# Experts' stage of a perceiver kernel: the routing weight multiplied into the result, and the routing placed between the first units

## The reference

```python
scores = einsum('btd,de->bte', x, router_w)
probs = softmax(scores)
routing_weights, routing_idx = top_k(probs, 2)
routing_weights = routing_weights / sum(routing_weights)
expert_w = einsum('btke,btk->bte', one_hot, routing_weights)
gate = einsum('bted,edf->btef', dispatched, gate_proj)
up = einsum('bted,edf->btef', dispatched, up_proj)
acts = silu(gate) * up
expert_out = einsum('btef,efd->bted', acts, down_proj)
return einsum('bted,bte->btd', expert_out, expert_w)
```

## Time and profile before

| | us |
|---|---|
| median of 3 runs | 3089.42 |
| lowest and highest | 3085.68, 3090.41 |
| the profiled execution, its own time | 3081.74 |
| its span, first to last instruction | 3080.0 |
| busy in the span: PE, DVE, ACT, POOL | 2488.2, 2267.4, 1868.9, 902.2 |
| mean granted TensorE clock | 0.882 of 2.4 GHz |

### The profile page before, as it was taken

The page is one execution under the profiler, slowest core; times in us unless marked ns, Lnnn a source line. Parts: engine busy times, 40 slices in busy tenths (PEclk is TensorE's granted clock), DMA queues, the critical chain, the costliest instruction groups (busy, mean ns, idle before and its releaser), DMA issues. The chain is left out here.

```text
span 3080.0 us, 35217 instructions
## 1 busy us (share of the span) xinstructions
PE 2488.2 (81%) x11867; PEld 1402.0 (46%) x11875; DVE 2267.4 (74%) x3046; ACT 1868.9 (61%) x2572; POOL 902.2 (29%) x498
## 2 busy tenths in 40 slices
PE   6699999998899999999999999954366641435998
PEld 3366666663344444444444444322355521423665
DVE  4487777754999999999999999855899921534443
ACT  4365555545888888888888889842455520013443
POOL 1021111111444444444444444300200031102665
PEclk9899999999999999999999999975667775557999
DMA  1000000001000000000000000000011013010000
GB/s 53 11 25 15 18 18 14 14 8 69 1 0 35 1 35 0 34 0 35 0 34 0 35 0 0 0 11 16 10 35 34 21 36 49 5 29 33 16 16 14
DMA packets 17732, 60.16 MB, mean 20 GB/s; under 512 B 1520, under 2 KB 10032, under 8 KB 15664
## 3 DMA queue, kind: packets, MB, share of 16 engines
q1 hardware_dynamic: 17584, 58.29, 6.2%
HBM read 53.04 MB, written 5.24 MB: 19 GB/s over the span
## 5 line engine op out<-in xcount | busy, mean ns | idle before, releaser
L251 PE MATMUL a_ps<-a_x,a_w 128*128 128x512 f32 x1536 | 695.6, 598 | 24.7 <-DVE a_kf L599 12.4
L251 PEld LDWEIGHTS a_ps<-a_x,a_w 128*128 128x128 f32 x1536 | 291.5, 191 | 404.3 <-issue 367.8
L774 POOL TENSOR_TENSOR a_den<-a_qf,a_ksum 128x1024 f32<-128x1024 f32 x128 | 271.2, 2119 | 510.2 <-DVE a_qf L592 473.5
L777 POOL TENSOR_TENSOR a_num<-a_qf,a_kvsum 128x1024 f32<-128x1024 f32 x128 | 295.0, 2304 | 186.1 <-DVE a_kvsum L617 186.0
L2137 DVE TENSOR_REDUCE x_rn<-x_sqk 128x8 f32<-128x512 f32 x256 | 174.3, 681 | 104.8 <-ACT x_sqk L2061 100.6
L2061 ACT ACTIVATE x_sqk<-x_b_k 128x512 f32<-128x512 f32 x256 | 153.1, 598 | 155.8 <-PE x_b_k L1973 149.3
L262 PE MATMUL a_ps<-a_att,a_w 128*128 128x512 f32 x480 | 215.8, 592 | 0.0
L592 DVE SCALAR_TENSOR_TENSOR a_qf<-a_eq,a_qf 128x1024 f32<-128x1024 f32 x128 | 195.4, 1526 | 1.7
L1954 POOL TENSOR_TENSOR x_kn<-x_craw,x_w 128x256 f32<-128x256 f32 x64 | 47.1, 736 | 509.7 <-DVE x_craw L2126 488.1
L445 ACT ACTIVATE a_den<-a_den,consts 128x1024 f32<-128x1024 f32 x128 | 147.0, 1149 | 57.3 <-POOL a_den L774 57.3
L599 DVE SCALAR_TENSOR_TENSOR a_kf<-a_ek,a_ps 128x1024 f32<-128x1024 f32 x128 | 155.5, 1215 | 27.8 <-ACT a_ps L441 23.1
(11 more groups left out here) (417 smaller groups left out, 5480.3 us busy)
## 6 DMA issues: line engine op xcount, KB each, us to landing
a_w<-layers SPq DMA_DIRECT2D x8, 2577.0 KB, 9.2
x_craw<-ctx SPq DMA_DIRECT2D x32, 256.0 KB, 2.6
y_cx<-ctx_t SPq DMA_DIRECT2D x16, 512.0 KB, 3.2
m_w<-experts SPq DMA_DIRECT2D x8, 608.0 KB, 3.8
x_w<-xattn_w SPq DMA_DIRECT2D x1, 2048.0 KB, 7.3
x_all<-x_t SPq DMA_DIRECT2D x1, 1024.0 KB, 4.9
t_scratch<-t_tmp SPq DMA_DIRECT2D x1, 1024.0 KB, 3.9
t_q<-t_scratch SPq DMA_DIRECT2D x4, 256.0 KB
```

The lines of the kernel that those rows point to most:

```text
L251: last = nc.tensor.matmul(bank(tile, j), col(par, part * HK + u * P, P), x[:, t0:t0 + BANK], start=True, stop=True)
L774: nc.gpsimd.tensor_tensor(by_batch(den[:, b, :]), by_batch(qf[:, b, :]), bcast(ksum[:, b, :], S), ALU.mult).then_inc(d_ready, 1)
L777: nc.gpsimd.tensor_tensor(by_batch(num[:, b, :]), by_batch(qf[:, b, :]), bcast(kvsum[:, b, :], S), ALU.mult).then_inc(n_ready, 1)
```

## The change

Seven things are done, all in `l1_moe` and its packing of weights.

1. The weight is multiplied into the result. `output(k)` on VectorE is now two instructions: `m_share` = `tile_o` x `m_wb` (L1284), then `x_all` += `m_share` (L1286), with a wait between. `spread`, `weigh`, `m_xw` and its two splits go. Gate and up both read `m_xn_hi`, `m_xn_lo`.
2. The weights reach all partitions through memory: SP writes `m_wt` (8 x 2048) to `m_scratch` once, and for each unit loads half a row back to 128 partitions (`weights_of`, 512 KB, 16 times).
3. The place of `tile_w` in PSUM serves a second `tile_u`; chunk n uses `tile_u[n % 2]`.
4. The selecting matrix goes from the experts' weights: 1088 columns instead of 1216.
5. The routing block and the experts' block become one. TensorE makes the scores and goes straight on with unit 0; VectorE's routing steps stand between its first multiplications; the turns (`turn`) stand after chunk 1 of unit 1, with the scores and the turned weights in `tile_o`.
6. The split weights of expert e are needed by unit 2e, one whole unit after they are made. The tokens are split in four pieces.
7. The loops are written out.

```diff
-E_SELECT = 2 * EF + 3 * D
-ECOLS = E_SELECT + P
+ECOLS = 2 * EF + 3 * D
...
-        tile_g, tile_u, tile_o, tile_w = banks = [ctx.enter_context(nc.psum_tensor(f"m_ps{i}", [P, HALF], F32))
-                                                  for i in range(4)]
+        tile_g, tile_u0, tile_u1, tile_o = banks = [ctx.enter_context(nc.psum_tensor(f"m_ps{i}", [P, HALF], F32))
+                                                    for i in range(4)]
+        tile_u = (tile_u0, tile_u1)
+        scratch = nc.dram_tensor("m_scratch", (EXPERTS, TOK), F32, kind="Internal").ap()
...
+                def weights_of(k):
+                    wait_past(sp, weighed, k - 1)
+                    half = k % 2
+                    sp.dma_start(wb[:, half, :], scratch[k // 2:k // 2 + 1, half * HALF:(half + 1) * HALF].broadcast_to([P, HALF])
+                                 ).then_inc(wb_loaded[half], 16)
...
+                def expert(e):
+                    sp.wait_ge(w_lo_done, e - 1)
+                    sp.dma_start(w[:, e % 2, :], dram["experts"][e]).then_inc(e_loaded[e % 2], 16)
...
+                sp.wait_ge(w_kept, 2)
+                sp.dma_start(scratch, wt[:, :]).then_inc(w_stored, 16)
+                sp.wait_ge(w_stored, 16)
+                for k in range(2):
+                    weights_of(k)
+                for k in range(2, UNITS):
+                    if k % 2 == 0 and k // 2 + 1 < EXPERTS:
+                        expert(k // 2 + 1)
+                    weights_of(k)
...
+                def turn(i):
+                    if i == 0:
+                        pe.wait_ge(weights_set, 1)
+                    else:
+                        pe.wait_ge(w_kept, i)
+                    for t in range(TILES // 2):
+                        last = nc.tensor.transpose(tile_o[0:EXPERTS, t * P:(t + 1) * P], prob[:, i * (TILES // 2) + t, :], ident)
+                    last.then_inc(w_turned, 1)
...
+                def gate_up(k, c):
+                    par, half = place(k)
+                    f0, fn = ECH[c]
+                    n = 3 * k + c
+                    if c == 0 and half == 0:
+                        pe.wait_ge(w_lo_done, k // 2 + 1)
+                    if c == 0 and k < 2:
+                        pe.wait_ge(xn_lo_done, 2 * k + 2)
+                    wait_past(pe, silu_done, n)
+                    for j in range(2):
+                        last = product(bank(tile_g, j)[0:fn], weights(par, E_GATE + f0, fn), (xn_hi, xn_lo),
+                                       slice(half * HALF + j * BANK, half * HALF + (j + 1) * BANK))
+                    last.then_inc(g_ready, 1)
+                    wait_past(pe, hid_done, n - 1)
...
+                def down(k):
+                    par, half = place(k)
+                    pe.wait_ge(hid_lo_done, 3 * k + 3)
+                    if k == 0:
+                        pe.wait_ge(w_kept, 2)
+                    wait_past(pe, weighed, k)
...
+                for k in range(2, UNITS):
+                    gate_up(k, 0)
+                    gate_up(k, 1)
+                    down(k - 1)
+                    gate_up(k, 2)
+                down(UNITS - 1)
...
+                for k in range(UNITS):
+                    for c in range(3):
+                        silu(k, c)
+                        if 3 * k + c:
+                            hid_high(3 * k + c - 1)
+                        if k == 1 and c == 1:
+                            keep(0)
+                            keep(1)
+                    if k == 0:
+                        split_weights(1)
+                    elif k % 2 == 0 and k // 2 + 1 < EXPERTS:
+                        split_weights(k // 2 + 1)
...
+                def output(k):
+                    half = k % 2
                     t = slice(half * HALF, (half + 1) * HALF)
+                    dve.wait_ge(down_done, k + 1)
+                    dve.wait_ge(wb_loaded[half], 16 * (k // 2 + 1))
+                    wait_past(dve, added, k)
+                    nc.vector.tensor_tensor(share[:, :], tile_o[:, :], wb[:, half, :], ALU.mult).then_inc(weighed, 1)
+                    dve.wait_ge(weighed, k + 1)
+                    nc.vector.tensor_tensor(x_in[:, t], x_in[:, t], share[:, :], ALU.add).then_inc(added, 1)
```

More of the change, by code:

```diff
@@ L1064, in l1_moe @@
[L1064 to L1108, removed]
@@ L1111, in bank @@
+        hid_hi_done, hid_lo_done = sem("hid_hi_done"), sem("hid_lo_done")
         def bank(ap, j):
             return ap[:, j * BANK:(j + 1) * BANK]
[L1114 to L1124, removed]
+        UNITS = 2 * EXPERTS
@@ L1126, in l1_moe, with place @@
+        def place(k):
+            return k // 2 % 2, k % 2
         with nc.Block() as block:
@@ L1142, in product @@
                     return last
[L1144 to L1154, removed]
@@ L1177, in down, with route @@
-                def down(k, par, half):
+                def route():
+                    pe.wait_ge(r_loaded, 16)
+                    for t in range(TILES):
+                        last = nc.tensor.matmul(tile_o[:, t * EXPERTS:(t + 1) * EXPERTS], xn[:, t * P:(t + 1) * P],
+                                                router[:, :], start=True, stop=True)
+                    last.then_inc(scores, 1)
+                def turn(i):
[6 more added lines that the diff above has]
+                    last.then_inc(w_turned, 1)
@@ new lines, in gate_up @@
+                def gate_up(k, c):
[12 more added lines that the diff above has]
+                    wait_past(pe, hid_done, n - 1)
+                    for j in range(2):
+                        last = product(bank(tile_u[n % 2], j)[0:fn], weights(par, E_UP + f0, fn), (xn_hi, xn_lo),
+                                       slice(half * HALF + j * BANK, half * HALF + (j + 1) * BANK))
+                    last.then_inc(u_ready, 1)
@@ L1185, in down @@
                     last.then_inc(down_done, 1)
-                pe.sem_inc(down_done, 1)
-                pe.wait_ge(xn_lo_done, 2)
-                spread(0, 0, 0)
-                all_units(pe, unit, down)
+                route()
+                for c in range(3):
+                    gate_up(0, c)
+                gate_up(1, 0)
+                gate_up(1, 1)
+                turn(0)
+                turn(1)
+                gate_up(1, 2)
+                down(0)
+                for k in range(2, UNITS):
[3 more added lines that the diff above has]
+                    gate_up(k, 2)
@@ new lines, in _ @@
+                split_tokens(0)
+                split_weights(0)
+                split_tokens(1)
+                shift_scores()
+                split_tokens(2)
+                split_tokens(3)
+                rank_start()
+                dve.wait_ge(exped, 1)
+                steps.done(normalise())
+                rank_by(1)
+                hidden(0, 0)
+                for s in (2, 3, 4):
+                    rank_by(s)
+                hidden(0, 1)
+                for s in (5, 6, 7):
+                    rank_by(s)
@@ new lines, in _ @@
+                choose()
+                normalise().then_inc(weights_set, 1)
+                hidden(0, 2)
+                split_weights(1)
+                for c in range(3):
+                    hidden(1, c)
+                output(0)
+                for k in range(2, UNITS):
+                    hidden(k, 0)
+                    hidden(k, 1)
+                    output(k - 1)
+                    hidden(k, 2)
+                    if k % 2 == 0 and k // 2 + 1 < EXPERTS:
+                        split_weights(k // 2 + 1)
@@ L1292, in pack_moe @@
+                output(UNITS - 1)
 def pack_moe(a):
```

182 lines of the change are left out of this document (75 added, 107 removed).

## The result

The changed kernel takes 3039.42 us (median of 4 runs, 3028.96 to 3043.31), against 3087.55 for the kernel before beside it (4 runs, 3083.45 to 3090.41). The ratio is 0.984, with a 95% interval of 0.9812 to 0.9868: faster by 1.6%. The profiled execution took 3041.42 us, with a span of 3039.6.

The account below looks back on a forecast made before the run. Bound: TensorE's 928 matmuls plus waits. Start to 2823.3, plus units 175.4 + 12.0, plus tail 12.1 + 2.5, ends the stage at 3025.3 instead of 3074.6; 3089.4 - 49.3 = 3040 us, range 3031 to 3057.

Parts of the forecast that it names:

- The start: Scores to end of down(0): unit 0 starts at 2795.1, 25.9 us earlier, and down(0) ends at 2823.3.
- The term for a wait at up of (1,1): Unit 1, chunk 1: VectorE ends the third `m_hid` at 2809.7, just when TensorE's up product wants it.
- Rival 2: Units: the addition's two SBUF operands meet `m_hid_lo`, delaying down products 0.8 us each; 11 us, 3051; chance 0.05.
- The turns and ScalarE's copy: Before down(0): turns add 3.6 us to TensorE's path, and waiting for ScalarE's copy between their halves adds 1.4.
- The clock and the matmuls at each restart: Start: 90 matmuls at 0.232 us take 20.9, and the low clock after the scores costs 2.3.
- The units: Down(0) to last up product: 756 matmuls, 175.4 us, plus 12.0 of waits before down products (six 1.2, eight 0.6).
- The tail: Last up product to stage's end: unchanged chain of 12.1 us, then 2.5 for two instructions and a wait.
- The first load: First broadcast weights land at 2822.7, before down(0) ends at 2823.3; some 5 us of lateness would cost nothing.
- Rival 1: Units: the clock falls at the new waits; 14 us more (3054) if half do, 28 (3068) if all; chance 0.2.
- Rival 4: Down products: GpSimd's chain is covered, so the 12.0 us of waits go, giving 3028; chance 0.05.
- Rival 5: Units: broadcast loads are the bound; slower than before once a load takes 33 us; chance 0.02.
- rival 3: Start: routing between first units holds TensorE up (5 us) or first weights come late (13); 3045 to 3053; chance 0.1.

Follow-up runs that it names:

- `fill4`: Changed kernel plus four matmuls with overwritten result after chunk 0 of units 2 to 15; stage 241.4 us against 241.8.
- experiment 6: Changed kernel with GpSimd's first `m_hid_lo` held until the routing weights are set; stage 236.6 us against 241.8.
- `late_down`: Changed kernel with the previous unit's down product behind chunk 2 instead of chunk 1, and `output` behind the third `m_hid`; 3020.52 us, ratio to before 0.9777.
- `late_fill4`: `late_down` plus the four extra matmuls of `fill4` in each unit; stage 234.3 us against 222.3 in `late_down`.
- `warm_tail`: Changed kernel plus 16 matmuls with no use after the last up product; stage 242.5 us against 241.8.
- experiments 1 to 3: `fill4`, `late_down` and `late_fill4`: extra matmuls on the changed kernel, its down product later, then both; stages 241.4, 222.3 and 234.3 us.
- `late_one_u`: `late_down` with a single accumulator for the up product; stage 235.5 us against 222.3 in `late_down`.
- `combined`: `late_down` with GpSimd also held until the routing weights are set; 3010.36 us, ratio to before 0.9750.

## Why the prediction was right, and where its sizes were off

Forecast 3040, measured 3039.42; the sign and the mechanism held. The agreement to within 1 us is luck. The stage shrank by 43.1 and not by 49.3, and scatter elsewhere made up for these 6.2 us: before had a median of 3087.55 in this comparison, 1.9 under the one that the forecast started from, and the medians' difference of 48 is 5 more than the stage gives.

**The start** was mis-sized by 3.5 us. "Down(0) ends 2823.3" is 33.6 after the first score matmul; measured 37.1.
- The scores took 6.8, not 5.4, at a clock of 0.50; in `fill4` they took 5.1. I took one execution's number for a constant: +1.4.
- VectorE "has the weights set at 2808.4 and ends the third `m_hid` at 2809.7, just when up of (1,1) wants it": the weights were set 23.8 us after the first score matmul and not 18.7. Of these 5.1 us, 1.4 are the scores' and 3.3 the two ranking steps' (1.39 and 2.31 instead of 0.20 and 0.21). The term for a wait at up of (1,1) was 0 and measured 2.65 (the gap of 2.88 less 0.23). The step that failed is that the 10.0 us of routing in the earlier trace rows keep their length when GpSimd works beside them; experiment 6 shows that they don't. Rival 2 had the right lock and the wrong instruction: I asked only whether the addition meets `m_hid_lo`, and it never does (all 16 take 1.22 or 1.23 us). The Trainium skill (SBUF — State Buffer, section on the two separate sides) states the rule for any VectorE operation with two SBUF inputs against a GpSimd operation that reads SBUF; 0.20 against 2.31 us is what it makes here of a short step.
- The turns and ScalarE's copy were put at 5.0 and took 3.6: -1.4. The 3.57 of the earlier trace rows is 16 turns at the lower clock, 0.21 us apart; here they are 0.11 apart, and 8 take 0.8. In `late_down`, `late_fill4` and `warm_tail` the turns are slow again, so this gain was not certain either.
- The clock and the matmuls at each restart take the rest, +0.9: 13 slow matmuls were 2.9, not 2.3.

**The units** were right: 187.4 forecast, 189.1 measured. The waits of 0.6 and 1.2 came out as 0.65 and 1.21, eight and six of them, and each is ended by `m_hid_lo` as the sum had it; experiments 1 to 3 show that the cover is what was lost. The missing 1.7 us are mostly 33 starts at gate and up products that come some 0.05 us late each.

**The tail** was 15.6, not 14.6. The chain is the same, and the low clock hit more of the last 18 matmuls (13; before has 9).

**The first load:** "`output(0)` doesn't wait" was wrong. The load lands 0.9 us after down(0) ends. It cost nothing, as the 5 us of room in the prediction had it.

**Rival 1 (the clock falls at the new waits)** didn't happen: 14 waits of 0.5 to 1.1 us and a granted clock of 1.00. **Rival 4** was wrong, as `late_down` shows what "covered" would look like. **Rival 5** was far off: loads land in 3.8 us, not 33. Of rival 3, a part came true: the 2.5 us at (1,1).

What the forecast didn't say is where the units' 19.5 us come from. Of before's 182.4 us in 12 units, 161.2 are matmuls (with 48 of `spread`) and 21.2 are waits and low clock; after, 150.1 and 12.8. So 11.1 come from the matmuls and 8.4 from waits and clock. Before's 21.2 are 8.9 for the six waits for `m_w_lo`, 3.6 for 18 slow matmuls and some 8.7 in gaps of 0.1 to 0.25 us where an accumulator or an operand changes; after's 12.8 are 11.1 at the down products and 1.7 in such gaps.

## What to carry to other kernels

Work that is taken out of an in-order engine was also time in which others caught up: before counting its length as gain, find the operand that the next instruction waits for, and look whether an independent piece can be put in between; here one exchange of order gave 19.5 us more, with no instruction taken away. When small VectorE steps with two SBUF operands are moved into a stretch where GpSimd works, add up to the length of one GpSimd instruction for each that runs beside them, and not only their own length: two of them added 3.3 us here. A second buffer is worth what its wait is worth after the larger one has gone: 1.0 us in one order, 10.0 in the other.

## What the runs showed of the hardware

- VectorE's steps with two SBUF operands on 32 or 48 columns take 0.20 us alone and up to 2.31 beside a GpSimd `tensor_tensor` of 2.40; `m_w_lo` goes from 1.28 to 2.59, and GpSimd's next instruction from 2.4 to 2.96. With one operand in PSUM (`m_hid`) or without an overlap (`x_all`) VectorE's 1024 columns take 1.22.
- Idle time of 1.41 us ahead of the last down product was followed by no slow matmul in `late_down`, `late_one_u`, `late_fill4` and `combined` (18 in 4.42 us in the chains of the first and the last), 1.80 in `warm_tail` by 8 matmuls at the lower clock, from the fifth on, and 5.45 in the other kernels by a slow start. With one run of the middle length, no limit between them can be read off.
- The number of slow matmuls behind the first gate is 5, 7, 12 or 13 in kernels whose start is alike, the scores take 5.1 us in `fill4` and 6.8 in the others of these, and the turns are 0.11 or 0.21 us apart. No edit explains it, and how the chip comes to one or the other stays open. It is not a plain sum: with 5 and 7 slow matmuls (`warm_tail`, `fill4`) TensorE waits longer for VectorE, and from the first gate product to the start of the last matmul of down(0) they take 32.4 and 30.3 us, against 30.1 with 13.
